# Experts' stage of a two-layer kernel: fp32 products split into three one-pass products, offsets loaded eight at a time

## What is computed

```python
s = softmax(raw_scores + expert_biases)          # raw_scores = u @ centroids.T, 16 columns
topk_vals, topk_idx = top_k(s, 2)
g_topk = sum(one_hot(topk_idx, 16) * topk_vals[..., None], axis=-2)
xe = einsum('bsd,eod->bseo', u, Wr) + br         # 16 experts
routed = einsum('bse,bseo->bso', g_topk, xe)
```

## Time and profile before

| | |
|---|---|
| median of 3 runs | 3075.06 us (3073.83 to 3078.61) |
| profiled execution | 3078.73 us, its span 3077.0 us |
| PE busy | 2815.2 us, 91% of the span |
| DVE, ACT, POOL busy | 2054.1, 1833.8, 2000.9 us |
| granted clock of TensorE, mean | 0.950 of 2.4 GHz |

### The profile page before, as it was taken

One profiled execution on the slowest core, in us unless ns is written; L12 is line 12 of the kernel. 1 busy time (PEld: TensorE's weight loads), 2 busy tenths in 40 slices (PEclk: granted clock), 3 DMA queues, 4 the chain that ended last, 5 costly groups with the idle time before them and its releaser, 6 DMA issues.

```text
span 3077.0 us, 46364 instructions
## 1 busy us (share of the span) xinstructions
PE 2815.2 (91%) x13026; PEld 2038.8 (66%) x13026; DVE 2054.1 (67%) x3489; ACT 1833.8 (60%) x2635; POOL 2000.9 (65%) x1246
## 2 busy tenths in 40 slices
PE   6999688655489999999999999999999999999997
PEld 4555366444356777777777777777777777777775
DVE  6887322388866676767676666667676667766763
ACT  4555112122257777777676767777777777777774
POOL 4777500277437777777777767777777777777775
PEclk8999899865589999999999999999999999999998
DMA  4432355588622232222222222232322222232321
GB/s 136 137 123 91 127 183 185 186 268 250 213 67 65 44 80 47 74 53 67 69 52 72 53 66 61 59 77 45 76 50 70 57 64 63 58 76 44 79 47 47
DMA packets 271650, 282.97 MB, mean 92 GB/s; under 512 B 97344, under 2 KB 214336, under 8 KB 271424
## 3 DMA queue, kind: packets, MB, share of 16 engines
q1 hardware_dynamic: 259264, 248.25, 30.2%
q0 software_dynamic: 12288, 33.57, 3.5%
HBM read 131.76 MB, written 82.31 MB: 70 GB/s over the span
## 4 chain that ended last, share of the span: by engine, by line
PE 68%; ACT 1%; DVE 1%; DMA 1%; POOL 1%; issue 1%; SPq 0%; POOLq 0%; ACTq 0%; DVEq 0%
PE psV_b L1532 7%; PE psV_b L1527 7%; PE psV_b L1528 7%; PE psS_b L1515 7%; PE psS_b L1514 7%; PE psN_b L1500 7%; PE psY_b L1455 4%; PE psX_b L1455 4%; PE psY_b L1456 4%; PE psY_b L1457 4%; PE psX_b L1456 4%; PE psX_b L1457 4%; POOL pp_lo_b L1245 1%; DMA xT_lo<-xT_lo_dram 1%; PE psN_b L1584 0%
## 5 line engine op out<-in xcount | busy, mean ns | idle before, releaser
L1245 POOL TENSOR_TENSOR pp_lo_b<-pf_b,pp_hi_b 128x1024 fp32r<-128x1024 f32 x512 | 1228.6, 2400 | 609.2 <-ACT pp_hi_b L1287 523.5
L1391 DVE TENSOR_REDUCE negmax_b<-psN_b 128x2 fp32r<-128x1024 f32 x512 | 626.7, 1224 | 379.2 <-PE psN_b L1500 371.5
L1282 ACT ACTIVATE pf_b<-psS_b 128x1024 f32<-128x1024 f32 x512 | 525.7, 1027 | 239.9 <-PE psS_b L1515 236.8
L1514 PE MATMUL psS_b<-qA_b,kA_b 128*128 128x512 f32 x1024 | 405.8, 396 | 6.6 <-DVE qB_b L1406 4.8
L1515 PE MATMUL psS_b<-qB_b,kB_b 68*128 68x512 f32 x1024 | 406.3, 397 | 0.0
L1528 PE MATMUL psV_b<-pp_hi_b,vals_lo_b 128*64 128x512 f32 x1024 | 403.5, 394 | 0.0
L1527 PE MATMUL psV_b<-pp_hi_b,vals_hi_b 128*65 128x512 f32 x1024 | 402.1, 393 | 1.4
L1500 PE MATMUL psN_b<-kA_b,qA_b 128*128 128x512 f32 x1024 | 322.6, 396 | 4.6 <-DVE negmax_b L1391 4.5
L1306 ACT ACTIVATE kA_b<-psX_b 64x512 fp32r<-64x512 f32 x256 | 151.7, 593 | 290.3 <-PE psX_b L1457 285.5
L1532 PE MATMUL psV_b<-pp_lo_b,vals_hi_b 128*65 128x512 f32 x1024 | 320.1, 394 | 5.0 <-POOL pp_lo_b L1245 5.0
L1287 ACT ACTIVATE pp_hi_b<-pf_b 128x1024 fp32r<-128x1024 f32 x256 | 271.5, 1060 | 8.1
(11 more groups left out here) (201 smaller groups left out, 5394.5 us busy)
## 6 DMA issues: line engine op xcount, KB each, us to landing
kA_b<-kA_b SPq DMA_DIRECT2D x128, 256.0 KB, 3.0
qB_b<-qA_b SPq DMA_DIRECT2D x128, 256.0 KB, 2.9
inverse_b<-inverse_dram SPq DMA_DIRECT2D x256, 128.0 KB, 3.0
xs_e<-rows_dram SPq DMA_DIRECT2D x144, 128.0 KB, 2.0
results_dram<-ys_e SPq DMA_DIRECT2D x72, 256.0 KB, 2.3
x_a<-x_dram SPq DMA_DIRECT2D x16, 512.0 KB, 4.8
part_dram<-acc_a SPq DMA_DIRECT2D x32, 256.0 KB, 2.1
acc_s<-part_dram SPq DMA_DIRECT2D x32, 256.0 KB
```

The source lines that it names most:

```text
L1245: pool.tensor_tensor(pp[1][:, c], pf[:, c], pp[0][:, c].bitcast(F32), ALU.subtract).then_inc(pl_pool, 1)
L1282: a.activation(pf[:, c], psS[:], ACT.Exp).then_inc(exp_act, 1)
L1391: v.tensor_reduce(negmax[:, n.slot(2), 2 * c:2 * c + 2], psN[:], AX.X, ALU.max, negate=True).then_inc(mx_dve, 1)
L1514: pe.matmul(psS[:, t], kA[:, s, keys], qA[:, s], start=True, stop=False)
```

## The change

Three things change together.

1. *Products.* Rows are loaded, turned and multiplied in the type fp32r. ACT writes the high part of the turned rows in fp32r; DVE subtracts it from PSUM and writes the low part; PE's products of a pair wait for that subtraction (`t_dve`) and not for ACT's copy. Each fp32 product becomes three fp32r products: high rows by high weights, high rows by low weights, low rows by high weights.
2. *Weights.* The split of the weights is made in routing: ACT copies one chunk of 128x512 into `wr_hi` at the end of each of the steps 4 to 19, and DVE, after the last of its steps, subtracts all 16 chunks in place. A second identity, `ident_r`, is made at the start.
3. *Offsets.* The class `Offsets` loads the offsets of eight jobs into eight registers by one instruction, one group of eight ahead of its use, on SP, PE and DVE. The two instructions behind each single load, which test the value's bounds, are gone.

The core of the diff:

```diff
+                if 4 <= v < 20:
+                    at = weights_of_experts(v - 4)
+                    a.wait_ge(raw_in, 16 * (v - 3))
+                    a.activation(wr_hi[at], raw[at], ACT.Copy).then_inc(wr_act, 1)
...
+            for c in range(16):
+                at = weights_of_experts(c)
+                v.wait_ge(wr_act, c + 1)
+                v.tensor_tensor(raw[at].bitcast(F32R), raw[at], wr_hi[at].bitcast(F32), ALU.subtract).then_inc(wr_dve, 1)
...
-        xs = sb("xs", [P, XS, D])
-        xt = sb("xt", [P, 2, U, KD, P])
+        wr = [wr_hi, raw[:].bitcast(F32R)]
+        xs = sb("xs", [P, XS, D], F32R)
+        xt = [sb(f"xt_{p}", [P, 2, U, KD, P], F32R) for p in ("hi", "lo")]
...
-        def where(eng, j):
-            return eng.value_load(kept.table[0:1, 2 * P + j:2 * P + j + 1], min_val=0, max_val=rows.shape[0] - P)
+        GROUP = 8
+        class Offsets:
+            def load(self, g):
+                n = min(GROUP, jobs - g * GROUP)
+                if n > 0 and g not in self.held:
+                    at = self.first + g * GROUP
+                    self.held[g] = nc.values_load_multi_w_load_instructions(
+                        kept.table[0:1, at:at + n], engines=[self.engine], min_val=0, max_val=self.most,
...
+            def ahead(self, j):
+                if j % GROUP == 0:
+                    self.load(j // GROUP)
+                    self.load(j // GROUP + 1)
...
+                    source.ahead(j)
                     need(sp, t_pe, 1, (j - XS) // U, 1)
-                    sp.dma_start(xs[:, j % XS], rows[bass.ds(where(sp, j), P), :]).then_inc(x_in[j % XS], 16)
+                    sp.dma_start(xs[:, j % XS].bitcast(F32), rows[bass.ds(source[j], P), :]).then_inc(x_in[j % XS], 16)
...
-                a.activation(flat(xt[:, n % 2]), psT[:, n % 2], ACT.Copy).then_inc(t_act, 1)
+                a.activation(flat(xt[0][:, n % 2]), psT[:, n % 2], ACT.Copy).then_inc(t_act, 1)
...
             for n in range(PAIRS + 1):
+                if n < PAIRS:
+                    need(v, t_act, 1, n, 1)
+                    v.tensor_tensor(flat(xt[1][:, n % 2]), psT[:, n % 2], flat(xt[0][:, n % 2]).bitcast(F32), ALU.subtract).then_inc(t_dve, 1)
                 m = n - 1
                 if m >= 0:
-                    at = [v.value_load(kept.table[0:1, m * U + t:m * U + t + 1], min_val=0, max_val=(NE - 1) * D) for t in range(U)]
+                    weights.ahead(m * U)
+                    at = [weights[m * U + t] for t in range(U)]
...
-                need(pe, t_act, 1, n, 1)
+                need(pe, t_dve, 1, n, 1)
                 need(pe, y_dve, U, n - 3, U)
                 for t in range(U):
                     j = n * U + t
-                    at = pe.value_load(kept.table[0:1, j:j + 1], min_val=0, max_val=(NE - 1) * D)
+                    at = weights[j]
                     out = psY[:, n % 3, t * D:(t + 1) * D]
                     for k in range(KD):
-                        mm = pe.matmul(out, xt[:, n % 2, t, k], raw[:, k, bass.ds(at, D)], start=(k == 0), stop=(k == KD - 1))
+                        left = [part[:, n % 2, t, k] for part in xt]
+                        right = [part[:, k, bass.ds(at, D)] for part in wr]
+                        pe.matmul(out, left[0], right[0], start=(k == 0), stop=False)
+                        pe.matmul(out, left[0], right[1], start=False, stop=False)
+                        mm = pe.matmul(out, left[1], right[0], start=False, stop=(k == KD - 1))
```

More of the change, by code:

```diff
@@ L96, in __init__ @@
         self.ident = sb("ident_f", [P, P])
+        self.ident_r = sb("ident_r", [P, P], F32R)
         self.wtern = sb("wtern", [P, KD, D], F32R)
@@ L105, in need, with route @@
         eng.wait_ge(sem, per * n + k)
-def route(nc, io, rows, part, region, jobs, kept, raw, raw_in):
+def route(nc, io, rows, part, region, jobs, kept, raw, wr_hi, raw_in):
     x_dram = io["x"].rearrange("(g t p) d -> g p t d", t=TB, p=P)
@@ L671, in _, with experts @@
                     pe.matmul(psB[:, 0, 0:1], masks[:, 2], delta[:, 0:1], start=True, stop=True).then_inc(tern_pe, 1)
-def experts(nc, io, rows, results, region, jobs, kept, raw, raw_in):
+def experts(nc, io, rows, results, region, jobs, kept, raw, wr_hi, raw_in):
     with ExitStack() as ctx:
@@ L703, in experts, with __init__, __getitem__ @@
         block = ctx.enter_context(nc.Block())
-        def where(eng, j):
-            return eng.value_load(kept.table[0:1, 2 * P + j:2 * P + j + 1], min_val=0, max_val=rows.shape[0] - P)
+        GROUP = 8
+        class Offsets:
+            def __init__(self, engine, first, most):
+                self.engine, self.first, self.most, self.held = engine, first, most, {}
+            def load(self, g):
[4 more added lines that the diff above has]
+                        kept.table[0:1, at:at + n], engines=[self.engine], min_val=0, max_val=self.most,
+                        skip_runtime_bounds_check_because="the tables are made from counts and clamped on the chip", bass_reorder=False)[1]
+            def ahead(self, j):
+                if j % GROUP == 0:
+                    self.load(j // GROUP)
+                    self.load(j // GROUP + 1)
+            def __getitem__(self, j):
+                return self.held[j // GROUP][j % GROUP]
         out_dram = results.rearrange("(n t p) d -> n p t d", t=U, p=P)
@@ L772, in turn @@
                             at = (t * KD + k) * P
[L773 removed]
+                            mm = pe.transpose(psT[:, n % 2, at:at + P].bitcast(F32R), xs[:, j % XS, k * P:(k + 1) * P], kept.ident_r[:])
                     mm.then_inc(t_pe, 1)
+            weights = Offsets(mybir.EngineType.PE, 0, (NE - 1) * D)
+            weights.ahead(0)
             turn(0)
[L777 removed]
             for n in range(PAIRS):
+                weights.ahead(n * U)
                 turn(n + 1)
[L780 removed]
+                need(pe, t_dve, 1, n, 1)
                 need(pe, y_dve, U, n - 3, U)
@@ L1610, in two_layers @@
                 raw = hold.enter_context(nc.sbuf_tensor("wr_raw", [P, KD, NE * D], F32))
+                wr_hi = hold.enter_context(nc.sbuf_tensor("wr_hi", [P, KD, NE * D], F32R))
                 raw_in = hold.enter_context(nc.semaphore("wr_raw_in"))
-                route(nc, io, rows, part, region, jobs, kept, raw, raw_in)
-                experts(nc, io, rows, results, region, jobs, kept, raw, raw_in)
+                route(nc, io, rows, part, region, jobs, kept, raw, wr_hi, raw_in)
+                experts(nc, io, rows, results, region, jobs, kept, raw, wr_hi, raw_in)
             settle(nc, io, results, part, xT_hi, xT_lo, base, early, kept)
```

20 lines of the change are left out of this document (11 added, 9 removed).

## The result

The changed kernel takes 3048.26 us (median of 4 runs, 3046.26 to 3050.40) beside 3076.84 us for the kernel before on the same chip: a ratio of 0.990, 95% interval 0.9892 to 0.9915, so about 29 us less. Forecast were 42 us less and 3033 us; 3048 lies inside the range of 3008 to 3060, though not in its main case of 3019 to 3044.

What follows compares the result with a forecast made beforehand. Experts' stage bound together by TensorE, SP's queue and a loop over four pairs. Terms: -45 + 4.2 + 0.2 - 1 = -42 us, from 3075 to 3033 us; main case 3019 to 3044 (0.56), range 3008 to 3060.

Steps and rivals of the forecast that it cites:

- Term 4: Start of the experts' stage: TensorE no longer waits for the first value load, biases come earlier; gain 1 us.
- rival B: Experts' stage: the load of eight offsets is dear, 1.9 us, 2.5 us a pair, 3054 us; chance 0.14.
- Term 1: Pace of the experts' stage: from 2.84 to 2.20 us a pair over 71 steps, 45 us less.
- L: Experts' stage: the load of eight offsets by one instruction, taken at 0.7 us, bounds 0.58 and 4.6 us.
- Rival D: Experts' stage: transfers crowd, row landing grows from 2.0 to 3.5 us, 2.6 us a pair, 3061 us; chance 0.08.
- rival E: Experts' stage: TensorE's clock falls to the low level, 3.4 us a pair, 3118 us; chance 0.06.
- All three limits lie within 0.25 us [...], so only a change that lowers all three helps: Experts' stage before: TensorE 2.72, SP 2.69, loop over four pairs 2.6 us a pair, beside the measured 2.84.
- The products' 0.5 us: TensorE in the experts' stage: twelve one-pass products take 1.37 us a pair against 1.85 for eight fp32 records.
- DVE's new wait, costed at nothing: Experts' stage: ACT's copy and DVE's subtraction before a product, 1.4 us, covered by other work; uncovered up to 1.4 us a pair.
- Term 2: Routing: ACT's copies delay each of 8 even steps by about 0.5 us, 4.2 us more; bounds 0 and 10 us.
- Term 3: End of routing: DVE's 16 subtractions, some 10 us, cost nothing, with 6 us of cover left.
- The signs named ahead: First to last drain 156 us, SP waiting for DVE in most pairs, DMA share 0.75 to 0.8, clock 1.00, routing later.

Runs made afterwards that it cites:

- before_on_act: The kernel before, with single value loads and fp32 products, with only the stores of results moved to ScalarE's queue, two pairs later: 3038.37 us, ratio 0.989.
- offsets_only: The kernel before with only the group loads of offsets added, fp32 products kept: 3042.16 us, ratio 0.989.
- split_only: The kernel before with only the new routing work (weight copies, subtractions, second identity), fp32 products kept: 3077.88 us, ratio 1.0010.
- stores_on_act: The changed kernel, eight slots, with the stores of results moved from SP's to ScalarE's queue, two pairs later: 3004.53 us, ratio 0.977 of before.
- group2: The changed kernel with offsets loaded in groups of two values in place of eight: 3046.15 us, ratio 0.991.

## Why the prediction came out as it did

**Direction and place: right.** The gain lies in the experts' stage, mostly in the pace, and the start gave 1.5 us in the one trace (Term 4 said 1). The main case, 3019 to 3044 us, was missed by 4 us. The time lies next to rival B's (3049 to 3054), but B's dear group load is not the cause.

**Term 1, the pace: mechanism right for a usual pair, mean mis-sized.** Its pieces after the change: the group load 0.56 us (0.7 taken); one-pass products 0.119 us apart (0.115); four fp32r transposes 0.35 us up to the first product (0.45); two row loads from the store 1.1 us (1.05); landing 2.6 us (2.0). With these the loop is 0.14 + 0.75 + 0.03 + 1.1 + 2.6 + 2 x (0.35 + 1.43 + 0.1) = 8.4 us, 2.1 a pair, and L/4 makes 2.24; the median interval was 2.15. Term 1's size failed where it took a usual pair for the mean: the 11 long intervals added 0.3 us a pair. Rival D (landing) and rival E (low clock) each came true in part, E only behind pauses and for about a pair each time. The allowance for both was 0.08 us.

**"All three limits lie within 0.25 us [...], so only a change that lowers all three helps": wrong.** It rested on reading 2.72 us as TensorE's own time. before_on_act leaves TensorE's list as it was, lowers SP's work and takes the store out of the loop, and gained 35 us. TensorE's own round was 2.16 us. The parts of the change bear it out: the offsets gave the whole gain, and the products none. That the offsets worked mostly through SP's queue is likely, as before_on_act gains as much with TensorE's and VectorE's value loads in place; no run groups SP's loads alone.

**The products' 0.5 us: worth nothing here.** 1.85 became 1.43 us, but TensorE's time was in the loop only twice in four pairs, and the longer landing (2.6 us, 2.3 in offsets_only) and the pauses took back what that gave. The usual pair was quicker by 0.09 us (medians 2.15 and 2.24), and the long intervals beyond it were 22 us in sum and not 12: offsets_only had a pace of 2.41, the whole 2.45. The subtraction is not the reason: the usual drain still started 0.42 us after the last product.

**L and rival B: right to reject.** The rule of the Trainium skill that a load costs about 200 ns for each register even in bulk ("Runtime: NRT & Kernel Launch", section "Instruction fetch mechanics") asks for an estimated 1.6 us; SP needed 0.56 us for eight and 0.54 for two. The page speaks of registers loaded from HBM, and this table lies in SBUF, so the rule may hold for its own case; no run here loads from HBM. Its other rule, a floor of about 600 ns for a load ("DMA: Bandwidth & Descriptors", section "Latency and other measured facts"), agrees.

**DVE's new wait, costed at nothing: right in the main.** TensorE's waits of 368 to 560 us have one row for it:

```profile
PE psY_e L834 <- DVE xt_lo_e L790: 0.7, 2, 0.4
```

VectorE waits for ScalarE's copy 45 us in sum (52 times), and TensorE's products hardly wait for VectorE.

**Term 2, ACT's copies in routing: its first half right, its sum not borne out.** 4.2 us were charged. TensorE's waits for the delayed tanh did grow, before (first row) and after (second; one more of 1.8 us stands at L439), from 60 to 350 us, and its wait at the choosing chain fell from 10.5 us (third):

```profile
PE psG_a L596 <- DVE th_a L433: 6.3, 3, 2.3
...
PE psG_a L609 <- DVE th_a L442: 6.8, 10, 2.3
...
PE psC_a L621 <- DVE mask_a L480: 9.1, 14, 0.8
```

So the hidden product waited 11 times in place of 3, and 2.3 us more in sum: the eight even steps at about 0.3 us, near the 0.34 us reckoned past the cover. The chain behind did not pass that on, and all of TensorE's waits of that stretch together came to 20.9 us against 20.0. In the traces routing ended at the same time (367.83 and 367.98 us); the interval of split_only, 0.3 to 5.8 us, leaves a cost of some us open.

**Term 3, the 16 subtractions: right.** They ran unbroken and ended at 358.58 us, before SP's last transfers of routing.

```profile
348.87 9.71 DVE L593 TENSOR_TENSOR wr_raw<-wr_raw,wr_hi 128x512 fp32r<-128x512 f32 x16
```

**The sum.** Term 1 gave 71 x (2.84 - 2.45) = 28 us instead of 45, Term 2 about nothing instead of 4.2 the other way, the rest about 2. That Term 2 was charged and did not come made the miss smaller by those 4 us: luck.

**The signs named ahead.** SP's queue did wait for drains at most stores (45 times, 49.8 us, from 385 to 550 us), and VectorE's subtractions ended in time. First to last drain took 174 us and not 156, the DMA share was 0.69 and not 0.75 to 0.8, the clock 0.94 and not 1.00, and routing did not end later.

## What to carry to other kernels

Look first at what stands in one queue: a load for later behind a store that waits for now binds the lead to the work. In the changed kernel, moving the store to another engine's queue took another 42 to 44 us off, when the change itself had given 29; in the kernel before the same move gave 35, there mostly because SP's full queue had one issue less. A gap behind a wait is not the engine's own cost: before adding it to a floor, find the same instructions where the engine did not wait. And shorten an engine's work only once nothing holds its inputs: with the long lead one-pass products gave 17 us, before that nothing that shows. The best version run, stores_on_act, takes 3004.53 us, 0.977 of before.

## What was not expected of the hardware

- Loading two or eight values into registers took SP the same 0.54 to 0.56 us.
- Rows landed after 2.0 us (median) at a DMA share of 0.58, after 2.1 (group2), 2.3 (offsets_only) and 2.6 us (the changed kernel, before_on_act) at 0.69 to 0.71, and after 3.9 at 0.91. So the share alone doesn't set the landing time. At 0.91 TensorE was busy for 98% of the time at clock 1.00.
- After a stop of 2.6 us TensorE ran twelve products at 0.21 us each (1.2 GHz) and was back at 0.12 us (2.4 GHz) in the next pair; after a stop of 1.99 us it ran at 0.12 us throughout.
- Instructions come over the same DMA engines. Those of queue q8 are likely TensorE's, as it brought 11 packets in 165 us with three products for each and 8 in the same time with fp32 products (offsets_only). The Trainium skill ("Runtime: NRT & Kernel Launch", section "Instruction fetch mechanics") gives a refill in blocks of 16 KiB; 0.18 MB in 11 packets on q8 agrees, the packets of 8 KB on q14 do not.
- From one execution and chip to another the end of routing moved by several us with nothing of it changed (363.27 us in before_on_act, 367.98 in before). A few us between two single executions say little; the pace says more.
